# A three-attention decoder layer: fp32 probabilities and values in the third attention, a split in PSUM in the other two

## The reference

```python
x = layernorm(x + attn(x))                 # first attention: causal, LoRA-merged weights, output projection
h = mha(x, x, x)                           # second attention: self
y = ln(x + h)
h = mha(y, ctx, ctx)                       # third attention: cross, 750 keys
y = ln(y + h)
h = relu(y @ fc1 + b1) @ fc2 + b2
x = layernorm(x + ln(y + h))
x = layernorm(x + bitlinear_ffn(x))
# each mha and attn:
scores = einsum('bhqd,bhkd->bhqk', Q, K) / sqrt(32)
probs = softmax(scores, axis=-1)
ctx = einsum('bhqk,bhkd->bhqd', probs, V)
```

## Time and profile before

| | |
|---|---|
| device time, median of 3 runs | 3980.43 us (3968.77 to 3981.41) |
| profiled execution | 3972.95 us, span 3971.2 us |
| causal, self, cross, feed-forward | from 1, 741, 1413 and 2961 us of the span |
| PE busy, matmul | 84% of the span |
| PE busy, weight loads | 65% |
| DVE busy | 73% |
| ACT busy | 53% |
| POOL busy | 22% |
| granted PE clock, mean | 0.931 of 2.4 GHz |

### The profile page before, as it was taken

How to read it: one execution, slowest core, us unless ns; L and a number is a source line. 1 busy time by engine, 2 the same in 40 slices (tenths; PEclk the granted TensorE clock), 3 DMA queues, 4 the chain that set the end, 5 groups by cost and what they waited for, 6 DMA issues and landing times. The chain is left out here.

```text
span 3971.2 us, 99389 instructions
## 1 busy us (share of the span) xinstructions
PE 3341.3 (84%) x36576; PEld 2576.8 (65%) x36576; DVE 2893.3 (73%) x4907; ACT 2090.8 (53%) x4472; POOL 866.5 (22%) x802
## 2 busy tenths in 40 slices
PE   7999899588888748888888888988953999999996
PEld 4877778377677636777767777767732556565562
DVE  4767667477777847888888888888855566666666
ACT  2655555355555525666666666666644344343442
POOL 0211111044444500111112121111220212122121
PEclk9999999799989869999999999999956999999998
DMA  3333332233333332333323322323224000000000
GB/s 98 92 101 86 89 100 85 92 102 109 95 101 95 89 112 83 90 95 92 90 86 90 91 83 87 95 85 88 75 89 143 22 22 27 27 22 32 21 22 16
DMA packets 246179, 309.71 MB, mean 78 GB/s; under 512 B 108931, under 2 KB 166275, under 8 KB 245094
## 3 DMA queue, kind: packets, MB, share of 16 engines
q1 hardware_dynamic: 245734, 303.54, 25.7%
HBM read 212.45 MB, written 90.64 MB: 76 GB/s over the span
## 5 line engine op out<-in xcount | busy, mean ns | idle before, releaser
L798 DVE TENSOR_TENSOR cross_p_lo<-cross_p,cross_p_hi 125x448 f16<-125x448 f32 x768 | 559.2, 730 | 140.0 <-ACT cross_p_hi L736 134.7
L735 ACT ACTIVATE cross_p<-cross_ps 125x448 f32<-125x448 f32 x768 | 421.1, 548 | 421.7 <-PE cross_ps L693 406.6
L791 DVE TENSOR_REDUCE cross_mx<-cross_ps 128x1 f32<-128x750 f32 x512 | 475.8, 929 | 28.7 <-PE cross_ps L660 27.3
L736 ACT ACTIVATE cross_p_hi<-cross_ps 125x448 f16<-125x448 f32 x768 | 418.9, 545 | 0.0
L660 PE MATMUL cross_ps<-cross_qk_stack 96*128 96x375 f16 x1024 | 259.2, 335 | 126.3 <-DVE cross_mx L791 125.5
L1244 PE MATMUL ffn_ps_f<-ffn_xt,ffn_f_hi 128*128 128x256 f16 x1792 | 301.8, 276 | 16.5 <-ACT ffn_ht L1316 11.5
L693 PE MATMUL cross_ps<-cross_qk_stack 97*125 97x224 f16 x1536 | 295.0, 275 | 19.1 <-issue 15.6
L585 PE MATMUL cross_ps<-cross_w_hi,cross_ct 128*125 128x128 f16 x3072 | 305.9, 225 | 0.0
L863 POOL TENSOR_TENSOR cross_o_sum<-cross_o_raw 128x256 f32<-128x256 f32 x64 | 41.6, 650 | 1184.9 <-ACT cross_o_raw L742 1184.9
L585 PEld LDWEIGHTS cross_ps<-cross_w_hi,cross_ct 128*125 128x125 f16 x3072 | 294.0, 141 | 0.3
L710 PE MATMUL cross_ps<-cross_vs,cross_p_hi 125*128 125x65 f16 x3072 | 289.2, 193 | 2.7 <-DVE cross_p_lo L798 1.7
(11 more groups left out here) (260 smaller groups left out, 9673.2 us busy)
## 6 DMA issues: line engine op xcount, KB each, us to landing
cross_spill<-cross_proj SPq DMA_DIRECT2D x64, 487.0 KB, 2.9
cross_c_rows<-ctx SPq DMA_DIRECT2D x48, 500.0 KB
cross_qk_stack<-cross_spill SPq DMA_DIRECT2D x128, 187.5 KB, 3.7
cross_qk_stack<-cross_spill SPq DMA_DIRECT2D x64, 243.5 KB, 3.1
causal_spill<-causal_proj SPq DMA_DIRECT2D x64, 224.0 KB, 1.9
causal_qk_stack<-causal_spill SPq DMA_DIRECT2D x256, 56.0 KB, 2.0
self_spill<-self_proj SPq DMA_DIRECT2D x64, 224.0 KB, 2.0
self_qk_stack<-self_spill SPq DMA_DIRECT2D x256, 56.0 KB, 2.0
```

What stands on the lines that cost most here:

```text
L735: act.activation(p32[:, n % 2, :], ps_st[0:KC, n % 2, 0:2 * T], ACT.Exp, scale=EXP_SCALE)
L736: act.activation(p_hi[:, n % 4, :], ps_st[0:KC, n % 2, 0:2 * T], ACT.Exp, scale=EXP_SCALE).then_inc(exp_done, 1)
L791: dve.tensor_reduce(mx[:, g, t, h:h + 1], ps_qk[:, :, 0:KT // 2], AX.XY, ALU.max).then_inc(max_done, 1)
L798: dve.tensor_tensor(p_lo[:, n % 4, :], p32[:, n % 2, :], p_hi[:, n % 4, :], ALU.subtract).then_inc(lo_done, 1)
```

## The change

`attention` gets an argument `full_slots`. The slots of a unit now alternate between two heads: `slot(n)` is 0 or 1, and heads of a slot class in `full_slots` are multiplied in fp32. Cross gets `(0, 1)`, all heads; causal and self get `()`, none.

In cross: ACT takes one exponential into `p_full` (fp32); there is no `p_hi`, no `p_lo`, and no DVE instruction for a slot. The values are kept in fp32 as `vf`, 33 columns a head: ACT scales half of the heads out of PSUM, DVE the other half. "values" has 4 fp32 products a slot instead of 8 fp16 ones. POOL's sum of high and low part is gone.

In causal and self: ACT writes `p_hi` first and then the fp32 exponential over its own input in PSUM; DVE reads it there for `p_lo`; `p32` is gone. The 8 products stay.

In all three: `ps_st` has three banks instead of two (`ST_RING`), and a bank is free for new scores when the probabilities made from it are ready. `ps_pv` has one bank instead of two, holds two heads of each batch, and is copied out twice a unit, at slot `HALF` and at slot 0 of the next unit. DVE's reciprocal and POOL's sum and scaling each become two instructions.

```diff
-        ps_proj, ps_qk, ps_st, ps_pv = (ps_all[:, 2 * n:2 * n + 2, :] for n in range(4))
+        ps_proj, ps_qk, ps_st = ps_all[:, 0:2, :], ps_all[:, 2:4, :], ps_all[:, 4:4 + ST_RING, :]
+        ps_pv = ps_all[:, 7, 0:2 * OW].rearrange("p (t v) -> p t v", t=2)
...
                 if n == 0 and (g > 0 or b.i is not None or b.first > 0):
-                    yield "evacuate", b + (g - 1) // G, (g - 1) % G, 0
+                    yield "evacuate", b + (g - 1) // G, (g - 1) % G, 1
+                if n == HALF:
+                    yield "evacuate", b, g, 0
...
+        def slot(n):
+            return n % HALF % 2
+        def head(n):
+            return n // HALF + 2 * slot(n)
+        def chunk(n):
+            return n % HALF // 2 * 2
+        def probabilities_ready(b, g, n):
+            if slot(n) in full_slots:
+                return exp_done, no(b, g, PAIRS, n + 1)
+            return lo_done, b.val(lambda k: G * k * PAIRS * N_SPLIT // 2 + split_no(g, n))
...
-                    wait(pe, exp_done, done_before(b, g, PAIRS, n, 2))
+                    wait(pe, *st_free(b, g, n))
...
+                    if n % HALF == 0:
+                        wait(pe, pv_evac, no(b, g, 2, n // HALF))
                     if n == 0:
-                        wait(pe, pv_evac, no(b, g, 1, 0))
                         pe.wait_ge(proj_free, b.val(lambda k: job_index[LAST_V, k, g] + 1))
-                    pe.wait_ge(lo_done, no(b, g, PAIRS, n + 1))
+                    pe.wait_ge(*probabilities_ready(b, g, n))
...
+                            if s in full_slots:
+                                last = pe.matmul(ps_pv[:, t, O_AT[s]:O_AT[s] + HD + 1], p_full[:, buf, at:at + P],
+                                                 vf[:, g, c, 2 * full_slots.index(s) + n // HALF, :],
+                                                 start=first, stop=final)
+                                continue
...
-                    wait(act, lo_done, done_before(b, g, PAIRS, n, 2))
                     wait(act, pv_done, done_before(b, g, PAIRS, n, 4))
-                    act.activation(p32[:, n % 2, :], ps_st[0:KC, n % 2, 0:2 * T], ACT.Exp, scale=EXP_SCALE)
-                    act.activation(p_hi[:, n % 4, :], ps_st[0:KC, n % 2, 0:2 * T], ACT.Exp, scale=EXP_SCALE
-                                   ).then_inc(exp_done, 1)
+                    scores = ps_st[0:KC, st_bank(g, n), 0:2 * T]
+                    if slot(n) in full_slots:
+                        act.activation(p_full[:, p_buffer(n), :], scores, ACT.Exp, scale=EXP_SCALE
+                                       ).then_inc(exp_done, 1)
+                    else:
+                        act.activation(p_hi[:, p_buffer(n), :], scores, ACT.Exp, scale=EXP_SCALE)
+                        act.activation(scores, scores, ACT.Exp, scale=EXP_SCALE).then_inc(exp_done, 1)
...
-                    act.wait_ge(pv_done, no(b, g, PAIRS, PAIRS))
+                    act.wait_ge(pv_done, no(b, g, PAIRS, HALF * (n + 1)))
...
-                    act.copy(o_raw[:, g % 2, :, :], ps_pv[:, :, 0:GH * VW]).then_inc(pv_evac, 1)
+                    act.copy(o_raw[:, g % 2, :, OW * n:OW * (n + 1)], ps_pv).then_inc(pv_evac, 1)
 ...
-                elif kind == "scores":
+                elif kind == "scores" and slot(n) in split_slots:
                     dve.wait_ge(exp_done, no(b, g, PAIRS, n + 1))
-                    dve.tensor_tensor(p_lo[:, n % 4, :], p32[:, n % 2, :], p_hi[:, n % 4, :], ALU.subtract
-                                      ).then_inc(lo_done, 1)
+                    buf = p_buffer(n)
+                    dve.tensor_tensor(p_lo[:, buf, :], ps_st[0:KC, st_bank(g, n), 0:2 * T], p_hi[:, buf, :],
+                                      ALU.subtract).then_inc(lo_done, 1)
...
-        lambda sems: attention(nc, sems, "cross", x2, ctx, x3, ca, [None] * 3, ca_bias, ln2, False),
+        lambda sems: attention(nc, sems, "cross", x2, ctx, x3, ca, [None] * 3, ca_bias, ln2, False, (0, 1)),
```

More of the change, by code:

```diff
@@ L48 @@
 VW = 2 * HD + 1
+ST_RING = 3
 FF = 2048
@@ L179, in vector, with attention @@
             dve.scalar_tensor_tensor(lo, stage, S_W, hi, ALU.mult, ALU.subtract).then_inc(self.w_lo_done, 1)
-def attention(nc, sems, tag, x_in, kv_in, x_out, w, loras, biases, norm, causal):
+def attention(nc, sems, tag, x_in, kv_in, x_out, w, loras, biases, norm, causal, full_slots):
     NB = x_in.shape[0]
@@ L194, in attention @@
     PAIRS = NCH // 2 * GH
+    HALF = PAIRS // 2
+    split_slots = [s for s in range(2) if s not in full_slots]
+    N_SPLIT, N_FULL = len(split_slots), len(full_slots)
+    O_WIDTH = [HD + 1 if s in full_slots else VW for s in range(2)]
+    O_AT = [0, O_WIDTH[0]]
+    OW = sum(O_WIDTH)
     st = ExitStack()
@@ L445, in no, with p_buffer, split_no, st_bank @@
             return b.val(lambda k: (G * k + g) * per_unit + n)
+        def slot(n):
[4 more added lines that the diff above has]
+            return n % HALF // 2 * 2
+        def p_buffer(n):
+            return n % 4 if N_SPLIT != 1 else n % 4 // 2
+        def split_no(g, n):
+            return (g * PAIRS + n) // (2 // N_SPLIT) + 1
+        def probabilities_ready(b, g, n):
+            if slot(n) in full_slots:
+                return exp_done, no(b, g, PAIRS, n + 1)
+            return lo_done, b.val(lambda k: G * k * PAIRS * N_SPLIT // 2 + split_no(g, n))
+        def st_bank(g, n):
+            m = g * PAIRS + n
+            return 1 if not cross and m == G * PAIRS - 1 else m % ST_RING
+        def st_free(b, g, n):
+            m = g * PAIRS + n
+            back = next(d for d in range(1, G * PAIRS) if st_bank(0, (m - d) % (G * PAIRS)) == st_bank(g, n))
+            if m < back and b.i is None and b.first == 0:
+                return exp_done, 0
+            past = m - back
+            return probabilities_ready(b + (past // (G * PAIRS)), past // PAIRS % G, past % PAIRS)
         def done_before(b, g, per_unit, n, ring):
@@ L728, in perform @@
                     act.wait_ge(proj_full, b.val(lambda k: job_index[kind, k, g] + 1))
[L729 to L730 removed]
+                    out, src = destination(kind, b, g, 0)[0], source(kind, b, g, bank)
+                    if kind[0] == "v":
+                        if N_FULL:
+                            c0, c1 = (0, min(4, NCH)) if kind == "v0" else (4, NCH)
+                            last = act.mul(vf[:, g, c0:c1, 0:2, 0:HD], slot_heads(src, full_slots[0:1]), RESPLIT)
+                        if N_SPLIT:
+                            last = act.mul(out, slot_heads(src, split_slots), RESPLIT)
+                        last.then_inc(proj_hi, 1)
+                    else:
+                        act.mul(out, src, job_scale(kind)).then_inc(proj_hi, 1)
```

110 lines of the change are left out of this document (68 added, 42 removed).

## The result

| | before | after |
|---|---|---|
| device time, median | 3980.47 us (4 runs) | 4254.55 us (4 runs, 4253.02 to 4274.28) |
| ratio, 95% interval | | 1.070 (1.067 to 1.074) |
| profiled execution, span | 3972.95, 3971.2 us | 4274.28, 4272.5 us |
| causal | 733 us | 733 us |
| self | 665 us | 649 us |

The change costs 274 us, 7%. All of the loss is in cross; self gives back a little. The two together say how far a phase may be read: about 20 us in cross, 10 in self.

A forecast was written before the change was run, and what follows sets the result against it. DVE was taken to bound cross, PE close behind. Cross +260 us, causal and self together -40, on 3973 gave 4193 for the profiled execution; the median 7 above, 4200 us, range 4080 to 4400.

The forecast's parts named there:

- Two loads of two cycles a column: Cross: each fp32 product runs as two loads of 128 columns, 107 ns each, 0.82 us a slot.
- The unit: One cross unit: PE work 18.4 + 7.1 = 25.5 us, plus 0.4 for small waits, 25.9 us.
- DVE and ACT off the path: Cross: DVE falls from 18.9 to about 10 us a unit, ACT from 15 to about 8.
- The first unit and the last ones: Cross: the first unit adds 7 us; the last two and the one ahead of them together add 18.
- The loop turns: Cross: five turns, each followed by a time at clock 0.50, cost 9 us each, 45 in all.
- Self: Self phase: -53 us from shorter `p_lo`, +6 for the second copy and second reciprocal.
- The part for `p_lo`: Self: long `p_lo` under POOL's instructions go once read from PSUM, gaining 53 us (30 to 75).
- Causal: Causal phase: +7 us for the second copy and second reciprocal, at 0.1 us a unit.
- one pass a load: Rival, cross: each fp32 load takes one pass, about 57 ns; kernel faster at 3890 us; chance 12%.
- no overlap: Rival, cross: fp32 load and product do not overlap, 135 ns, 1.08 us a slot; 4395 us; chance 12%.
- DVE stays: Rival, cross: the change does not take DVE's share off the path, so PE still waits; no chance given.
- The clock stays low: Rival, cross: after loop turns a quarter of the units run at 1.2 GHz, +390 us, 4590; chance 5%.

The follow-up runs named there:

- e2_wide: The changed kernel with each fp32 product in cross streaming 66 value columns instead of 33, same loads, wrong sums: 4227.64 us.
- e2_narrow: The changed kernel with fp32 products of four of six key chunks in cross loading 64 queries instead of 128, wrong sums: 4243.45 us.
- the second profile: Another profiled execution of the changed kernel, code unchanged: 4259.1 us of span; median of its runs 4254.69 us.
- e1_split_only: The kernel before with only the fp32 exponential written over the scores in PSUM, in causal and self alone: 3943 us, ratio 0.990.
- e2_split_all: The kernel before with only the fp32 exponential written over the scores in PSUM, in causal, self and cross: 3888 us, ratio 0.975.
- e1_none: The changed kernel with no head multiplied in fp32; cross gets the PSUM split, three score banks and two copies a unit: 3896 us, ratio 0.980.

## Why the prediction was right, and where its terms were off

The sign, the size and the reason held: forecast 4200 (4080 to 4400), measured 4254.55. By its steps:

- **Two loads of two cycles a column** (107 ns, and 194 ns for the record; worked out from four loads of a statement that ran twice in the trace of before). Right in kind, and 5 ns short: the records take 192 ns, and the starts are 213 ns apart at clock 0.50, as worked out, but 112 at 1.00. e2_wide and e2_narrow confirm it from both sides, the stream hidden and the price going by columns. For 0.82 us a slot the trace has 0.81 behind transposes and 0.86 behind a projection, 0.83 in the mean. The Trainium skill, "TensorE: Matmul & The Clock Gate", section "LDWEIGHTS (loading the stationary operand)", gives 107 ns for 128 columns and by the same rule 53 for 64; for fp32 the traces come near it (112 and 58), for the fp16 loads they do not (58 for 125 columns).
- **The unit**, 25.9 forecast, 26.2 measured. The twelve slots took 9.9 us for the 9.8 forecast. The scores' products took 113 ns each in the mean where the sum has 98, 0.4 us a unit, and the rest of the work 0.2 more; of the 0.4 us that I left for waits nothing was needed. That the two errors nearly cancel is luck; the 0.3 us that is left makes 18 us over 60 units.
- **DVE and ACT off the path.** Right: one wait of 0.6 us is left. They fell less far than forecast, to 11.4 and 9.9 us a unit for 10 and 8, which costs nothing beside PE's 26.2.
- **The first unit and the last ones.** +7 forecast, +11 measured; +18 forecast for the last three, and 23.0, 24.7 and 24.0 us are +25: the last two came out at the 24 forecast, and it is the one ahead of them, 23.0 for 16, that was mis-sized; it ran at clock 0.50 for 13.5 us.
- **The loop turns: the term that was mis-sized.** I gave them 9 us each, 45 in all. The five units behind them take 37.4, 42.8, 38.1, 38.5 and 41.9 us instead of 26.2, and the five ahead of them 28.6 to 29.3, together 82 us. PE stands no longer than before; what grew is the time at clock 0.50 that follows, 23 to 34 us in each of these units instead of 4 to 6 in the kernel before. In the second profile it is 13 to 36 us, and the ten units cost 67 us. I had named this mechanism as a rival with all-or-nothing terms (a quarter of the units at half the clock) and left it at 9 us otherwise; it came in the middle. With products twice as wide this time is 10 to 13 us in each of the five units (e2_wide).
- **Self, -47 forecast, -16 measured, -5 in the second profile.** The part for `p_lo` was about right in kind: no `p_lo` over 626 ns is left, and the split alone gave 35 us (e1_split_only), of the 53 I took and above the 30 that I gave as its lower end. What I had at 6 us for the rest costs 19 by the first profile and 30 by the second; 14 to 15 us of it are the second pause at the loop turns. No step of the prediction asked where the code lies.
- **Causal, +7 forecast**, -1 and -4 measured: the second copy costs nothing that shows.

The sum was 4193 us for the profiled execution, which took 4274: +260 in cross became +323 (and +302 in the second profile), -40 in causal and self became -17, and feed-forward took 5 us less. Of the 81 us between, 37 are the loop turns, 18 the units, 11 the first and the last units, and 31 self; causal and feed-forward take some back.

The rivals: *one pass a load* fell by the 192 ns (its 57 ns a load was not read from the transposes either, whose products start 107 ns apart, 0.43 us for four), *no overlap* by e2_wide, and *DVE stays* by the waits. *The clock stays low* was in part true, at the turns.

What the prediction did not see at all is that reading the full exponential from PSUM pays in cross as well, 55 us (e2_split_all), since there the fp32 products took its place. In the kernel before, cross's DVE was the bound, and 768 `p_lo` of 730 ns were within reach of 624 with no change on PE.

## What to carry to other kernels

Before trading two fp16 products for one fp32 product, count loads, not products or columns: here an fp32 product that is no transpose loads its stationary operand twice, at 112 ns for 128 columns each, and four of them took 0.81 to 0.86 us in the place of eight fp16 ones with 0.22. By these numbers it can pay only where each load serves a long stream, or where PE stands idle anyway; no run here shows such a case. Where DVE is the bound, look first at which of its operands can be read from PSUM in place: that gained 55 us in cross, with the same products on PE. And when a profile shows an engine that stands at a loop turn for nothing, compare it with a build whose code is only shifted, before explaining it by the change.

## What the runs showed of the hardware that I had not expected

- PE at a loop turn stood a second time, 1.7 us in the mean in one build and 3.0 in another, where the loop's code lay later in the program: 29 instructions more in the loop of the phase before brought it, 29 more in its own did not. PE went on 1.2 to 1.7 us after a packet of 16 KB of the instruction queue had landed, at the first pauses and the second.
- A fp32 product twice as wide made the program faster (4228 against 4255 us): the time at clock 0.50 in cross fell from 277 us (235 in a second profile) to 115.
- A change of the stationary operand's width between 128 and 64 columns cost about 0.1 us each way, as much as a load of 128 fp32 columns.
- The exponential written back over its own input in PSUM takes what it took into SBUF: 543 ns in the mean in cross of e1_none, against 545 for the fp16 one beside it and 548 for the fp32 one into SBUF before the change.
